# Wide self-attention in a fused decoder kernel: scores copied with their minimum into SBUF, score blocks placed behind the turns

## What is computed

```python
def _mha(x, y, wq, wk, wv, li1_w, li1_b, ...):          # here y is x
    q = jnp.einsum('bsc,hcd->bhsd', xn, wq)             # 16 heads, D = 32
    k = jnp.einsum('btc,hcd->bhtd', yn, wk)
    v = jnp.einsum('btc,hcd->bhtd', yn, wv)
    a = jax.nn.softmax(jnp.einsum('bhsd,bhtd->bhst', q, k) * D ** (-0.5), axis=-1)
    mask = (jnp.arange(t)[None, :] > jnp.arange(s)[:, None]).astype(a.dtype)
    a = a * mask                                        # after the softmax
    o = jnp.einsum('bhst,bhtd->bhsd', a, v)
    x_out = x + o.reshape(...) @ li1_w + li1_b
```

## Times and profile before

| | us |
|---|---|
| median of 3 runs | 2798.28 (2797.87 to 2806.37) |
| the profiled execution | 2795.5 |
| its span, first to last instruction | 2793.8 |
| TensorE busy in it | 2405.5 (86%) |
| VectorE busy | 2002.1 (72%) |
| ScalarE busy | 1641.1 (59%) |
| GpSimd busy | 1108.5 (40%) |

### The profile page before, as it was taken

How to read it: one execution, slowest core, us unless ns; L and a number is a source line. 1 busy time by engine, 2 the same in 40 slices (tenths; PEclk the granted TensorE clock), 3 DMA queues, 4 the chain that set the end, 5 groups by cost and what they waited for, 6 DMA issues and landing times. The chain is left out here.

```text
span 2793.8 us, 48818 instructions
## 1 busy us (share of the span) xinstructions
PE 2405.5 (86%) x16107; PEld 1793.3 (64%) x16107; DVE 2002.1 (72%) x4456; ACT 1641.1 (59%) x4541; POOL 1108.5 (40%) x1577
## 2 busy tenths in 40 slices
PE   5888888887987999979974997999999789998696
PEld 4666666666974666656642774666666567765585
DVE  6999999996335777758979463777776557767565
ACT  6777767772225888866654344777776256654211
POOL 4455785865641111112321312222220155522774
PEclk7999999989997999999986998999999889999798
DMA  8500000004750000000004000000000000000376
GB/s 333 231 1 1 7 10 5 12 7 135 223 159 33 2 2 2 2 16 1 2 1 68 7 1 19 2 1 2 2 1 1 27 1 1 1 1 15 102 225 198
DMA packets 74187, 129.80 MB, mean 46 GB/s; under 512 B 29129, under 2 KB 47633, under 8 KB 69842
## 3 DMA queue, kind: packets, MB, share of 16 engines
q1 hardware_dynamic: 62418, 103.46, 12.3%
q0 software_dynamic: 9216, 19.02, 1.9%
q10 hardware_dynamic: 2304, 4.20, 0.4%
HBM read 69.23 MB, written 57.41 MB: 45 GB/s over the span
## 5 line engine op out<-in xcount | busy, mean ns | idle before, releaser
L1218 DVE TENSOR_TENSOR_SCAN s_state<-s_decay,s_state 128x4096 f32<-128x4096 f32 x32 | 279.0, 8718 | 1.6
L1090 PE MATMUL s_ysumP<-s_state,ident 128*128 128x256 f32 x1024 | 253.6, 395 | 0.0
L2181 ACT ACTIVATE s5a_prob<-s5a_scoreP,s5a_nmax 128x256 f32<-128x256 f32 x512 | 235.5, 481 | 22.7 <-DVE s5a_nmax L2353 21.0
L930 ACT ACTIVATE s_decay<-s_delta,s_aneg 128x255 f32<-128x255 f32 x512 | 211.8, 495 | 53.2 <-POOL s_delta L756 53.0
L2181 ACT ACTIVATE s2s_prob<-s2s_low,s2s_nmax 128x128 f32<-128x128 f32 (+1 forms) x512 | 225.4, 448 | 1.6 <-DVE s2s_nmax L2350 1.6
L1090 PEld LDWEIGHTS s_ysumP<-s_state,ident 128*128 128x128 f32 x1024 | 199.1, 201 | 27.6
L2353 DVE TENSOR_REDUCE s5a_nmax<-s5a_scoreP 128x4 f32<-128x1024 f32 x128 | 156.1, 1220 | 67.3 <-PE s5a_scoreP L2269 65.1
L2350 DVE CUSTOM_DVE_ANT_0 s2s_low<-s2s_scoreP,s2s_mask 128x128 f32<-128x128 f32 (+1 forms) x512 | 151.8, 353 | 55.6 <-PE s2s_scoreP L2269 54.3
L997 PE MATMUL s_bcP<-s_bc,s_sel 96*128 96x256 bf16 x768 | 131.6, 309 | 67.5 <-DVE s_state L1228 49.0
L2364 DVE TENSOR_TENSOR s5a_probT<-s5a_probP,s5a_mask 128x768 f32<-128x768 f32 x128 | 122.5, 957 | 63.1 <-PE s5a_probP L2279 62.0
L1228 DVE TENSOR_TENSOR s_state<-s_state,s_bcP 128x1024 f32<-128x1024 f32 x128 | 149.2, 1215 | 17.5 <-PE s_bcP L997 15.4
(11 more groups left out here) (674 smaller groups left out, 6320.8 us busy)
## 6 DMA issues: line engine op xcount, KB each, us to landing
sorted<-blank SPq DMA_DIRECT2D x32, 1105.0 KB, 27.9
s_state<-in_m_w SPq DMA_DIRECT2D x40, 512.0 KB, 4.2
s5n_m_w<-in_m_w SPq DMA_DIRECT2D x40, 384.0 KB, 3.8
s_decay<-sorted SPq DMA_DIRECT2D x40, 130.0 KB, 2.6
s5n_m_xin<-sorted SPq DMA_DIRECT2D x40, 130.0 KB, 3.2
s4w_mats<-s_scratch SPq DMA_DIRECT2D x4, 1024.0 KB, 13.1
s_state<-parts SPq DMA_DIRECT2D x8, 256.0 KB, 6.7
s_state<-parts ACTq DMA_DIRECT2D x8, 256.0 KB, 7.1
```

The lines of the kernel that those rows point to most:

```text
L930: ins = nc.scalar.activation(decay[c][:, n, 1:], delta[:, c, 1:], ACT.Exp, scale=aneg[:, c, n:n + 1])
L1090: ins = nc.tensor.matmul(ysumP[:, c, :], ident[:], state[s][:, c, n, :], start=False, stop=(n == NS - 1))
L1218: nc.vector.tensor_tensor_scan(cells, flat(decay[c]), cells, 0.0, ALU.mult, ALU.add).then_inc(S["scanned"], 1)
L2181: ins = nc.scalar.activation(prob[i][:, h, a:b], (low[n % 3] if kind == "causal" else scoreP[i])[:, h, a:b], ACT.Exp, bias=nmax[:, p % 4, ...
```

## The change

For the wide kind, `maxes` becomes the fused form of the causal kind: four instructions per pair that negate the scores, copy them to SBUF (`low`, now in both kinds) and take the minimum. In place of the mask their second operand is `blank`, one column of zeros repeated over 256 elements. The exponentials read `low` with scale -1 in both kinds. Scores wait for `maxed` in both kinds. The scores of pair 0 of the first batch come ahead of the loop, and in the loop `scores(p+1)` stands behind `turn(p-1)` and ahead of the item of `AT_B`, on VectorE `maxes(p+1)` behind `turn_out(p-1)` and ahead of both takes. GpSimd clears `blank` at the start.

```diff
--- before.py
+++ after.py
@@ -1939,8 +1939,9 @@
         bv = sc.sb("bv", [P, 2])
         bvw = [sc.sb(f"bvw{i}", [P, P]) for i in range(2)]
         lnw = sc.sb("lnw", [P, 4])
-        low = [sc.sb(f"low{i}", [P, 2, CUT]) for i in range(3)] if kind == "causal" else None
+        low = [sc.sb(f"low{i}", [P, 2, CUT]) for i in range(3)]
         mask = sc.sb("mask", [P, 3 * P])
+        blank = sc.sb("blank", [P, 1])
         hs = [sc.sb(f"hs{s}", [P, TB, C]) for s in range(2)]
         cell = sc.sb("cell", [P, 2])
         xqT = sc.sb("xqT", [P, L])
@@ -2031,17 +2032,18 @@
 
         @block.gpsimd
         def _(pool):
+            pool.memset(blank[:], 0.0).then_inc(S["masks"], 1)
             if kind == "causal":
 
                 pool.memset(mask[:], 0.0).then_inc(S["masks"], 1)
-                pool.wait_ge(S["masks"], 1)
+                pool.wait_ge(S["masks"], 2)
                 own = mask[:].rearrange("p (m k) -> p m k", k=P)[:, 0:3:2, :]
                 pool.affine_select(out=own, in_=own, compare_op=ALU.is_ge, fill=NEG, base=0,
                                    pattern=[[0, 2], [-1, P]], channel_multiplier=1).then_inc(S["masks"], 1)
             else:
 
                 pool.memset(mask[:], 1.0).then_inc(S["masks"], 1)
-                pool.wait_ge(S["masks"], 1)
+                pool.wait_ge(S["masks"], 2)
                 two = mask[:, P:3 * P].rearrange("p (m q) -> p m q", q=P)
                 pool.affine_select(out=two, in_=two, compare_op=ALU.is_gt, fill=0.0, base=0,
                                    pattern=[[0, 2], [-1, P]], channel_multiplier=1).then_inc(S["masks"], 1)
@@ -2177,9 +2179,8 @@
                 ac.wait_ge(S["maxed"], n + 1)
                 for r, (a, b) in enumerate(CUTS):
                     for h in range(2):
-                        kw = dict(scale=-1.0) if kind == "causal" else {}
-                        ins = nc.scalar.activation(prob[i][:, h, a:b], (low[n % 3] if kind == "causal" else scoreP[i])[:, h, a:b], ACT.Exp,
-                                                   bias=nmax[:, p % 4, h, r:r + 1], accum_out=den[s][:, r, 2 * p + h:2 * p + h + 1], **kw)
+                        ins = nc.scalar.activation(prob[i][:, h, a:b], low[n % 3][:, h, a:b], ACT.Exp,
+                                                   bias=nmax[:, p % 4, h, r:r + 1], scale=-1.0, accum_out=den[s][:, r, 2 * p + h:2 * p + h + 1])
                 ins.then_inc(S["exped"], 1)
 
             def o_take(t, c):
@@ -2262,7 +2263,7 @@
                 if p == 4:
                     pe.wait_ge(used["Q1"], t + 1)
                     pe.wait_ge(used["K1"], t + 1)
-                wait(pe, S["maxed"] if kind == "causal" else S["exped"], t * PAIRS + p - 1)
+                wait(pe, S["maxed"], t * PAIRS + p - 1)
                 rows_of = lambda h: slice(64 * (p % 2) + 32 * h, 64 * (p % 2) + 32 * h + 32)
                 for r, (a, b) in enumerate(CUTS):
                     for h in range(2):
@@ -2311,19 +2312,20 @@
                 if n != "T":
                     pe.wait_ge(used["T"], 1)
                 make(n, 0, 0)
-            if LEAD:
-                scores(0, 0, 0)
+            scores(0, 0, 0)
             if bias:
                 pe.wait_ge(S["bo_ready"], 1)
             for t, s in batches(pe):
                 for p in range(PAIRS):
-                    new = following(t, s, p) if LEAD else (t, s, p)
-                    if new:
+                    new = following(t, s, p)
+                    if not WIDE and new:
                         scores(*new)
                     at(AT_A, t, s, p, make)
                     e = earlier(t, s, p, 1)
                     if e:
                         turn(*e)
+                    if WIDE and new:
+                        scores(*new)
                     at(AT_B, t, s, p, make)
                     e = earlier(t, s, p, 2)
                     if e and e[2] % 2 == 1:
@@ -2337,21 +2339,18 @@
         def _(ve):
             st = Steps(ve, S["step"])
             st.begin(0)
-            ve.wait_ge(S["masks"], 2)
+            ve.wait_ge(S["masks"], 3)
 
             def maxes(t, s, p):
                 i = p % 2
                 n = t * PAIRS + p
                 ve.wait_ge(S["scores"], n + 1)
-                wait(ve, S["exped"], n - 2 if kind == "causal" else n - 3)
-                if kind == "causal":
-                    for r, (a, b) in enumerate(CUTS):
-                        for h in range(2):
-                            ins = nc.vector.tensor_tensor_reduce(low[n % 3][:, h, a:b], scoreP[i][:, h, a:b], mask[:, a:b], -1.0, BIG, ALU.add,
-                                                                 ALU.min, nmax[:, p % 4, h, r:r + 1])
-                else:
-                    ins = nc.vector.tensor_reduce(nmax[:, p % 4, :, :].rearrange("p h r -> p (h r)"),
-                                                  scoreP[i][:].rearrange("p h (r k) -> p (h r) k", r=2), AX_X, ALU.max, negate=True)
+                wait(ve, S["exped"], n - 2)
+                for r, (a, b) in enumerate(CUTS):
+                    for h in range(2):
+                        shown = mask[:, a:b] if kind == "causal" else blank[:, 0:1].to_broadcast([P, b - a])
+                        ins = nc.vector.tensor_tensor_reduce(low[n % 3][:, h, a:b], scoreP[i][:, h, a:b], shown, -1.0, BIG, ALU.add,
+                                                             ALU.min, nmax[:, p % 4, h, r:r + 1])
                 ins.then_inc(S["maxed"], 1)
 
             def turn_out(t, s, p):
@@ -2395,19 +2394,20 @@
                 ve.wait_ge(S["values_out"], 1)
                 nc.vector.tensor_tensor(bo[:], bo[:], oP[:, 0, 0:C], ALU.add).then_inc(S["bo_ready"], 1)
                 ve.wait_ge(S["bo_ready"], 1)
-            if LEAD:
-                maxes(0, 0, 0)
+            maxes(0, 0, 0)
             for t, s in batches(ve):
                 st.begin(t)
                 for p in range(PAIRS):
-                    new = following(t, s, p) if LEAD else (t, s, p)
-                    if new:
+                    new = following(t, s, p)
+                    if not WIDE and new:
                         maxes(*new)
                     if p == 0 and not first(t):
                         recip(t - 1, 1 - s)
                     e = earlier(t, s, p, 1)
                     if e:
                         turn_out(*e)
+                    if WIDE and new:
+                        maxes(*new)
                     at(AT_A, t, s, p, take)
                     at(AT_B, t, s, p, take)
                     if p == 0 and not last(t):
```

## The result

The changed kernel takes 2902.64 us (median of 4 runs, 2895.44 to 2904.27) against 2801.01 us of the kernel before beside it. The ratio is 1.0356, with a 95% interval of 1.033 to 1.0381. It is 101.6 us slower; I had forecast 2863, with a range up to 2888.

A forecast was written before the change was run, and what follows sets the result against it. The wide self-attention was taken as bound by TensorE, busy 54.2 of 55 us. Terms 25.2 + 14.3 + 22.1 + 1.6 - 3.0 + 4.8 = 65.0 us on 2795.5, with 2.8 for the median, gave 2863, range 2850 to 2888.

The forecast's parts named there:

- Part 1: Scores wait for the maxima instead of the exponentials of pair n-2: worth nothing, as the turn ahead waits for those exponentials.
- Part 2: New order: VectorE's takes freeing bank itemP queue behind the maxima pass, so TensorE waits; three waits plus small terms.
- the three waits: TensorE per batch: K1 1.68 us (25.2 in all), Q1 0.95 (14.3), T 1.96 in place of 0.38 (22.1).
- The small terms: scores(4) waiting for ScalarE's release 1.6 us, R no longer behind ScalarE's take -3.0, turn(6) 4.8.
- the 4.8 of turn(6): Between T and turn(6), eight exponentials each 0.04 us slower from SBUF, 15 times: 4.8 us.
- Part 3: VectorE's fused maxima pass: four instructions take 1.38 us against 1.22 for the reduction; the repeated column is free.
- Part 4: ScalarE's exponentials start 0.49 us apart from SBUF, 0.45 from PSUM; 4.8 us ahead of turn(6), covered elsewhere.
- rival 1: TensorE's clock falls because of its new waits: up to 25 us more, 2875 to 2888; chance 0.12.
- The last of the prediction's own signs of being wrong: The stage's granted clock row falling under 1.00 would show the prediction wrong.
- Rivals 2: The repeated column slows VectorE's fused instruction: 61 us at half rate, half of the way 30 us, 2893; chance 0.05.
- Rival 3: TensorE doesn't wait for the takes; the earlier score block empties all its waits: -10 us, 2788; chance 0.04.
- 4: Nothing measurable moves in the stage, slack takes up the new waits: 2798; chance 0.04.

The follow-up runs named there:

- fused_only: Changed kernel's fused pass, SBUF exponentials and weaker wait, but TensorE and VectorE order of the kernel before; ratio to before 1.0027, stage 4.2 us longer.
- fill_all: Changed kernel with dummy transposes on TensorE in the waits of Q1, K1 and T; ratio to the kernel before 1.0230, stage 537.5 us.
- takes_first: Changed kernel with VectorE's takes of R0, R1 and L ahead of the maxima pass; ratio to the kernel before 1.0060, stage 490.2 us.
- order_only: Kernel before with the new TensorE and VectorE order, old reduction and exponentials from PSUM; ratio to before 1.0312, stage 546.7 us.
- l_first_pv: Kernel before with VectorE's take of L ahead of turn_out(3) and TensorE's pv ahead of R0 at p = 1; ratio to before 0.9992.
- fill_k1: Changed kernel with 13 dummy transposes in K1's wait alone, on another chip; ratio to the kernel before 1.0376, stage 571.2 us.

## Why the prediction was right or wrong

- Part 1 (the weaker wait is worth nothing): right as far as tested. With it and the old order `fused_only` gains nothing; no run takes it out of the new order by itself.
- Part 2, the three waits: right to some hundredths. K1 at S + 3.30 where I had 3.33, T at S + 3.04 where I had 3.03, Q1 at S + 3.33 where I had 3.33 to 3.43. The small terms too: `fused_only` has 4.2 us for the 4.8 of turn(6), and `fill_all` has 65.8 us for the sum of 65.0. What part 2 lays wholly on VectorE's queue is in part TensorE's own order: of K1's wait `takes_first` leaves 0.78 us.
- Part 3 (a pass of 1.38, the repeated column free): right. Starts are 0.35 and 0.34 apart, 420 ns each. By that, section 5.2 of the Trainium skill's Vector Engine (DVE) Microarchitecture Reference doesn't carry over to a repeated word, for which it has no measurement: read to the letter, it would have made the pass an estimated 0.69 us longer.
- Part 4: right, see `fused_only`.
- The result was wrong because rival 1 happened, and more than in full. The step that failed is the clock: the sum has no term for it, and the rival that had one was given a chance of 0.12 and at most 25 us (1.8 us in each of 14 batches). The trace of the changed kernel has 115 us of the stage at the lower level, 78 more than that of `fill_all`, and these cost 33.3 us (570.8 against 537.5 with the clock held), 2.4 a batch. The last of the prediction's own signs of being wrong, a clock row under 1.00, is what came.
- I had weighed the rival by the busy share of 20 us: 84% seemed covered by the stretch with 17.1 of 20 and a clock of 1.00. But the changed stage is busy 87% and still loses, and `order_only` has batches of 88% with a clock of 1.00. Such a share doesn't show that TensorE stands still for 1.6 or 1.9 us in one piece. That the length of the piece decides and not the share is not shown: no run changes the one without the other. The forecast should have been 65 and 25, near 2890, with the range beyond 2900.
- `order_only` shows that the loss by the clock isn't fixed by the program: 34.02 and 30.81 us a batch in one execution. The 78 us are what this execution drew; by their times, 2895 to 2904, the four runs of the changed kernel drew much the same.
- Rivals 2, 3 and 4 did not happen. Rival 3's 10 us of waits exist in the kernel before, but what wins some of them is a take moved forward: `l_first_pv` has 6.3.

What stays open: why filling K1's wait leaves as much time at the lower level as before while filling T's takes 34 us of it away, and what ended the dips in `order_only` at one batch. There the dips begin 34.13 us apart and the batches last 34.02, so that a dip moves by 0.1 us a batch against the waits. When a wait falls may thus count beside its length, but no run here tests it.

## What to carry to other kernels

An instruction that is moved ahead on one engine to give it slack moves everything behind it on the next engine: look for what is queued behind it there, above all if it frees a buffer that all others need. In a stage that is bound by TensorE, price a new wait of TensorE by its length, and keep a term for the clock beside it. In the changed kernel the waits and small terms cost 65 us and the clock 33 more; in a batch of `order_only` with a dip the two cost 3.3 and 3.2 us; in `takes_first`, where no wait leaves TensorE idle for more than 0.78 us, the clock cost nothing. If the waits can't be avoided, dummy matmuls can hold the clock, but here only with all three waits filled, and they win back the clock's part alone: `fill_all` is still 2.3% slower than the kernel before.

## What the runs showed of the hardware

- TensorE waits of 1.6 us (K1) and 1.9 us (T), each without the other but with Q1's 0.8 beside it, in an otherwise full stream brought the granted clock of the stage down to 0.95 and 0.91. In `order_only` 1.33 us (K1) and 1.65 us (T) did it together. It didn't happen in every batch: `order_only` and `fill_k1` have batches at 1.00 with the same waits. Waits of 0.78 us (K1 in `takes_first`, 15 times) left it at 1.00. The Trainium skill, TensorE: Matmul & The Clock Gate, section "HAM oscillation", describes such an oscillation for longer gaps; here shorter ones did it.
- At the lower level 78 us cost 33.3 us and not the half, 39. What takes up the rest isn't shown: TensorE was busy in all but 0.6 of the 78 us.
- The fused copy and minimum starts every 0.345 us at 256 columns and lasts 0.42, whether its second operand is a full mask or one column repeated.
